# Moving a feed-forward's opening into the attention before it, and turning a recurrence's first batches from resident tokens

## The chip, the cores and the metric

The kernel runs on one core of a Trainium2 chip. Its engines are TensorE (PE; its weight loads are listed as PEld), VectorE (DVE), ScalarE (ACT), GpSimd (POOL) and SyncE (SP), which issues most transfers. Each engine runs its own queue in order; they meet only through semaphores. The metric is the time of one execution on the device in microseconds; the median of the timed runs counts. A span is the time from the first to the last instruction of the profiled execution, and times in rows count from its start.

## The reference

A decoder of two layers over 8 batches of 256 tokens with 256 columns, f32. Each of six steps is added to its input and layer-normalised:

```python
x = _layernorm(x + _L0_attn_ref(x, ...))    # window attention
x = _layernorm(x + _L0_xattn_ref(x, ctx, ...))   # first cross attention, 77 context tokens
x = _layernorm(x + _L0_ffn_ref(x, ...))     # eight experts, one for each token
x = _layernorm(x + _L1_attn_ref(x, ...))    # convolution of 4 taps, gates, recurrence
x = _layernorm(x + _L1_xattn_ref(x, ctx, ...))   # second cross attention
x = _layernorm(x + _L1_ffn_ref(x, ...))     # feed-forward with binarised weights
```

The steps that matter here:

```python
# recurrence, its start:
gi = jnp.einsum('btd,hd->bth', x, W_in)
gate, xc = jnp.split(gi, 2, axis=-1)
# feed-forward (bw = mean|w| * sign(w) for each output):
h = jax.nn.gelu(jnp.einsum('bsd,hd->bsh', x, bw1) + b1, approximate=False)
out = jnp.einsum('bsh,dh->bsd', h, bw2) + b2
```

## The kernel before, in words

All tokens stay in SBUF in one tensor, X (in rows: tokens), 16 tiles of 128 tokens, two tiles (TPB) for each batch. Six stages run one after the other, each a block with its own program for each engine. A block ends when all engines have ended; only then does the next one's work begin. A matmul needs its contraction dimension on the partitions, so every stage first transposes a batch on PE, against an identity matrix, into PSUM. A product of f32 precision is made of f16 passes: a value is scaled, its rounded half is written by ACT ("high", names ending in h) and the rest by DVE ("low", ending in l).

**The experts leave their results in DRAM** (slots). The recurrence (L2163) gathers them by token: POOL's `fetch(b, par)` issues two indirect DMAs (L2286) into y. DVE's `enter(b, par)` (L2428) adds them to X and takes the statistics, POOL's `root_in` the root, and `enter_norm` writes the normalised tokens back to X, counting `norm_in.ln_done`. POOL's order at the start is fetch(0), fetch(1), root_in(0), root_in(1), fetch(2).

**The recurrence's opening.** SP's `stage(b, par)` (L2257) waits for `ln_done` of that batch and copies its two tiles from X to a buffer xs by DMA; `stage(0, 0)` and `stage(1, 1)` stand first, then `next_loads(sp)`, the four weight loads of the second attention (L838), then a loop over the other batches. PE: `turn(0, 0)` (L2552) transposes xs into one PSUM bank, ACT's `tokens` copies it out, `way_in(0)` (L2564) multiplies by w_in, ACT's `conv_input` (L2340) puts the result into padded, DVE's `convolve` (L2446) makes the convolution, and after `turn(1, 1)` the loop over batches starts. ACT begins the block with the four high parts of w_g (L2329). DVE makes the low parts (L2528, w_gl; each 128x1024 of w_g and w_gh), all four of them after enter and enter_norm of batches 0 and 1 and before `convolve(0, 0, 0)`.

**The attention's last batch.** `cross_attention` (L1018) goes through eight units a batch. In each, PE turns four heads' probabilities (`turn_probs`, L1315), ACT writes the high part (L1173) and the next unit's exponential (L1165), DVE the low part (L1216), PE weighs the values (`weigh`, L1329). At the end of a tile DVE takes a reciprocal (L1223) and normalises, PE transposes ("heads", L1286), ACT copies (L1158), PE multiplies by the output weights ("mix", L1291), DVE adds the residual (L1233) and takes statistics, POOL the root (L155), DVE writes X (L159). In the last batch units 5 to 7 have no next batch to prepare. There, and at named places behind the last unit ("weighed", "heads", "mix", "last"), `cross_attention` calls an object `follow`, which may put the next stage's first work into the score banks (`spare`) and the banks of turned probabilities (`turned`). The first attention's follow is `RouteStart`, the router's opening: it transposes pairs of tiles, writes their halves and multiplies. The second attention's is `Nothing`, whose methods are empty.

**The feed-forward's opening.** `binary_ffn` (L2689): SP `stage(0, 0)`, `stage(1, 1)` (L2746), then reloads when `x_turned` and `xb_ready` allow. POOL's `add_bias` (L2779) adds b2 to a batch's two tiles. PE: `turn(0, 0)` and `turn(1, 1)` (L2889) into one bank x_bank, the second after DVE's low part of the first; `way_up(0, 0)` (L2902): four banks of eight f16 passes of 128x256. ACT: `tokens` (L2798, high parts), `all_hidden(0, 0)`: Gelu (L2806) of each bank, then high parts of h (L2813). DVE: `tokens_low` (L2837), `low` (L2843). Then `all_batches`: PE's batch b is turn(b+2), way_up(b+1), way_down(b) (L2915, 32 passes); DVE's is tokens_low(b+2), two lows of b+1, `residual(b, ·)` (L2850, L2855) for two tiles, two more lows, and the two writes of y.

Of the kernel before, what the change touches and what calls it, by code (L numbers as in the profile page):

```python
# [993 lines left out]


class Nothing:


    def add_buffers(self, ctx, nc, tag):
        pass  # L1000

    def load(self, sp):
        pass

    def gpsimd(self, pool, X):
        pass

    def scalar(self, act, place, spare, turned, out):
        pass

    def vector(self, dve, place, spare):
        pass

    def tensor(self, pe, place, X, norm, spare, turned, out, ident):
        pass
# [1147 lines left out]
def recurrence(nc, gates, slots, slot, ident, half, X, next_loads, cross, ctx_dram):  # L2163


    with ExitStack() as ctx:
# [86 lines left out]
        def _(sp):  # L2253
# [5 lines left out]
            stage(0, 0)  # L2259
            stage(1, 1)  # L2260
# [158 lines left out]
        def _(dve):  # L2419
# [103 lines left out]
            for b in (0, 1):  # L2523
                enter(b, b)
                enter_norm(b)
            for j in range(HT):
                dve.wait_ge(g_high, j + 1)
                dve.scalar_tensor_tensor(out=w_gl[:, j], in0=w_g[:, j], scalar=SCALE, in1=w_gh[:, j],  # L2528
                                         op0=ALU.mult, op1=ALU.subtract).then_inc(g_low, 1)
            dve.wait_ge(cleared, 1)  # L2530
# [11 lines left out]
        def _(pe):  # L2542
            pe.wait_ge(gates.w_loaded, 48)

            def turn(b, par):

                pe.wait_ge(staged[par], 8 * (b - par) + 16)
                if not first(b):
                    pe.wait_ge(x_ready, b)
                for g in range(KT_):  # L2550
                    for t in range(TPB):
                        ins = pe.transpose(x_bank[:, g, t * P:(t + 1) * P], xs[par][:, t, g * P:(g + 1) * P], ident[:])  # L2552
# [136 lines left out]
def binary_ffn(nc, weights, ident, half, X, out):  # L2689

    with ExitStack() as ctx:
# [9 lines left out]
        xb = [sb(f"xb{k}", [P, TPB, DIM]) for k in range(2)]  # L2701
        xh = [sb(f"xh{k}", [P, KT_, SEQ], F16) for k in range(2)]
        xl = [sb(f"xl{k}", [P, KT_, SEQ], F16) for k in range(2)]
        h = sb("h", [P, FT, SEQ])
        hh = [sb(f"hh{k}", [P, FT, SEQ], F16) for k in range(2)]
# [11 lines left out]
        xb_ready = sem("xb_ready")  # L2717
        x_turned = sem("x_turned")
        x_high = sem("x_high")
        x_low = sem("x_low")  # L2720
        up = sem("up")
        h_ready = sem("h_ready")
        h_high = sem("h_high")
# [20 lines left out]
        def _(sp):  # L2744
# [14 lines left out]
            stage(0, 0)  # L2759
            stage(1, 1)  # L2760
            restage(0, 0)
            restage(1, 1)
# [10 lines left out]
        def _(pool):  # L2773
            def add_bias(b, par):
                pool.wait_ge(staged[par], 8 * (b - par) + 16)
                if not (isinstance(b, int) and b < 2):
# [258 lines left out]
```

## Time and profile before

| | us |
|---|---|
| median of 3 runs | 1252.14 (1252.08 to 1253.18) |
| the profiled execution, its own run | 1253.59 |
| its span | 1251.9 |
| PE busy | 1069.3 (85%) |
| DVE busy | 958.7 (77%) |
| ACT busy | 693.1 (55%) |
| POOL busy | 385.7 (31%) |

The rows come from one profiled execution. A row of a timeline is: start, duration, engine, line, operation, the tiles it writes and reads, their sizes, how many instructions were merged (x4), and in brackets the idle time before it and what ended that. Matmuls overlap: the distance between two starts tells their rate, the printed duration includes the last one's way out. An SP row merges issues that follow each other, so its duration tells little. The granted clock of TensorE is given as a share: 1.00 is 2.4 GHz, 0.50 is 1.2 GHz.

### The profile page before, as it was taken

The numbers are of one execution on the slowest core, as the hardware profiler recorded it, in microseconds if no ns is written. First come the engines' busy times: TensorE is split into PE (matmuls) and PEld (weight loads), VectorE is DVE, ScalarE is ACT, GpSimd is POOL, SyncE is SP. The second block draws the span as 40 slices with busy tenths as digits, with TensorE's granted clock in tenths as the row PEclk, the third lists the DMA queues.
The fourth block names the chain that finished last, engine by engine and source line by source line (L and its number), as shares of the span: only waits on it lengthen the run. The fifth ranks groups of instructions, "written<-read, shape, count | busy, mean of one in ns | idle before, by whom it ended". The sixth has DMA issues, their size and how long they took to land. (4 is left out here: it accounts for less than half of the span.)

```text
span 1251.9 us, 30100 instructions
## 1 busy us (share of the span) xinstructions
PE 1069.3 (85%) x10763; PEld 856.2 (68%) x10763; DVE 958.7 (77%) x2126; ACT 693.1 (55%) x1461; POOL 385.7 (31%) x538
## 2 busy tenths in 40 slices
PE   4899999999999799985379998489999669998696
PEld 3578878778777577764357776477788557776585
DVE  7588878877887598897838783669998659988397
ACT  2354444544555265555637775368788626555484
POOL 5023222222221255651310000523431326555132
PEclk9899999999999899996579999699999969999799
DMA  7000000200000320005515521300000000000011
GB/s 261 8 11 2 10 13 2 83 3 2 2 2 2 117 89 23 11 9 229 202 53 186 189 97 52 113 18 26 25 9 21 1 14 23 23 15 5 35 53 49
DMA packets 34071, 65.34 MB, mean 52 GB/s; under 512 B 7590, under 2 KB 23334, under 8 KB 30886
## 3 DMA queue, kind: packets, MB, share of 16 engines
q1 hardware_dynamic: 32422, 59.62, 13.5%
q0 software_dynamic: 1536, 4.20, 1.0%
q8 instruction: 73, 1.20, 0.4%
q14 instruction: 40, 0.33, 0.1%
HBM read 43.03 MB, written 12.39 MB: 44 GB/s over the span
## 5 line engine op out<-in xcount | busy, mean ns | idle before, releaser
L1173 ACT ACTIVATE ca_pth<-ca_turned 77x512 f16<-77x512 f32 x128 | 75.9, 593 | 101.7 <-PE ca_turned L1315 101.7
L395 ACT ACTIVATE wa_probs<-wa_scores,wa_minus_top 128x192 f32<-128x192 f32 x256 | 83.3, 437 | 80.8 <-DVE wa_minus_top L488 80.8
L1116 POOL TENSOR_TENSOR ca_z<-ca_z,ca_top 128x308 f32<-128x308 f32 x128 | 88.1, 701 | 113.5 <-DVE ca_top L1211 113.5
L351 POOL TENSOR_TENSOR wa_q<-wa_by_cos,wa_by_sin 128x256 f32<-128x256 f32 x32 | 23.4, 732 | 266.5 <-DVE wa_by_sin L483 266.5
L1216 DVE SCALAR_TENSOR_TENSOR ca_ptl<-ca_turned,ca_pth 77x512 f16<-77x512 f32 x128 | 87.0, 680 | 21.4 <-ACT ca_pth L1173 21.4
L1315 PE MATMUL ca_turned<-ident,ca_probs 128*77 128x128 f32 x512 | 87.0, 294 | 14.3 <-ACT ca_probs L1165 13.8
L406 ACT ACTIVATE wa_pth<-wa_turned 128x384 f16<-128x384 f32 x128 | 58.4, 506 | 72.2 <-PE wa_turned L715 72.2
L1315 PEld LDWEIGHTS ca_turned<-ident,ca_probs 128*77 128x77 f32 x512 | 57.4, 151 | 44.9 <-ACT ca_probs L1165 24.5
L640 PE MATMUL wa_scores<-wa_xh,wa_wh 128*128 128x256 f16 x256 | 70.4, 275 | 11.2 <-DVE wa_wl L467 9.1
L488 DVE TENSOR_REDUCE wa_minus_top<-wa_scores 128x2 f32<-128x384 f32 x128 | 62.3, 548 | 20.9 <-PE wa_scores L703 18.9
L715 PE MATMUL wa_turned<-ident,wa_probs 128*128 128x128 f32 x512 | 68.3, 275 | 7.8 <-ACT wa_probs L395 3.9
L1165 ACT ACTIVATE ca_probs<-ca_z 128x308 f32<-128x308 f32 x128 | 57.7, 451 | 23.2 <-POOL ca_z L1116 23.2
L640 PE MATMUL wa_scores<-wa_xl,wa_wh 128*128 128x256 f16 x256 | 70.5, 275 | 0.0
L640 PE MATMUL wa_scores<-wa_xh,wa_wl 128*128 128x256 f16 x256 | 70.5, 275 | 0.0
L536 DVE SCALAR_TENSOR_TENSOR wa_ptl<-wa_turned,wa_pth 128x384 f16<-128x384 f32 x128 | 64.9, 548 | 6.6 <-ACT wa_pth L406 6.6
L2580 PE MATMUL re_g<-re_convh,re_w_gh 128*128 128x256 f16 x256 | 69.8, 273 | 0.0
L2580 PE MATMUL re_g<-re_convl,re_w_gh 128*128 128x256 f16 x256 | 69.8, 273 | 0.0
L2580 PE MATMUL re_g<-re_convh,re_w_gl 128*128 128x256 f16 x256 | 69.8, 273 | 0.0
L2564 PE MATMUL re_in<-re_xt,re_w_in 128*128 128x256 f32 x256 | 61.8, 403 | 9.0 <-ACT re_xt L2333 9.0
L715 PEld LDWEIGHTS wa_turned<-ident,wa_probs 128*128 128x128 f32 x512 | 57.6, 141 | 15.4 <-issue 6.7
L2564 PEld LDWEIGHTS re_in<-re_xt,re_w_in 128*128 128x128 f32 x256 | 51.1, 202 | 18.8 <-issue 7.2
L2011 DVE SCALAR_TENSOR_TENSOR ex_hl<-ex_h,ex_hh 128x320 f16<-128x320 f32 x72 | 35.2, 488 | 37.5 <-ACT ex_h L1983 36.8
(368 smaller groups left out, 3649.4 us busy)
## 6 DMA issues: line engine op xcount, KB each, us to landing
ex_stage<-in_ew SPq DMA_DIRECT2D x16, 1024.0 KB, 6.8
slots<-slots_zeros SPq DMA_DIRECT2D x10, 512.0 KB, 6.1
ca_xs<-tokens SPq DMA_DIRECT2D x16, 256.0 KB, 2.4
ex_xe<-slots SPq DMA_DIRECT2D x11, 320.0 KB, 3.2
slots<-ex_y SPq DMA_DIRECT2D x9, 320.0 KB
wa_x_stage<-in_xt SPq DMA_DIRECT2D x8, 256.0 KB, 3.1
tokens<-in_x SPq DMA_DIRECT2D x1, 2048.0 KB, 15.3
ca_w<-in_xw SPq DMA_DIRECT2D x2, 1024.0 KB, 6.4
```

What stands on the lines that cost most here:

```text
L395: ins = act.activation(probs[2 * (u % 2) + t][:, h, t * WINDOW:t * WINDOW + SPAN], s_bank[i][:, t * SPAN:(t + 1) * SPAN], ACT.Exp, bias=mi ...
L406: act.activation(spans(pth[k][:]), spans(t_bank[h][:]), ACT.Copy, scale=PSCALE).then_inc(probs_high, 1)
L488: dve.tensor_reduce(minus_top[:, g % 2, i], s_bank[i][:, 0:2 * SPAN].rearrange("p (t s) -> p t s", t=2), AX.X, ALU.max, negate=True).then_ ...
L536: dve.scalar_tensor_tensor(out=spans(ptl[k][:]), in0=spans(t_bank[h][:]), scalar=PSCALE, in1=spans(pth[k][:]), op0=ALU.mult, op1=ALU.subtr ...
L640: ins = pe.matmul(bank[:, a * SEQ:(a + 1) * SEQ], weight[:, k, cols], x[:, par, k], start=(m == 0), stop=(m == 3 * KT_ - 1))
L715: ins = pe.transpose(t_bank[h][:, j * SEQ + t * P:j * SEQ + (t + 1) * P], probs[2 * (u % 2) + t][:, h, j * P:(j + 1) * P], ident[:])
L1116: pool.tensor_tensor(z[k][:, heads], z[k][:, heads], top[:, k, heads].unsqueeze(2).broadcast_to((P, UH, CTX)), ALU.subtract).then_inc(shif ...
L1173: act.activation(pth[k][0:CTX], t_bank[k][0:CTX], ACT.Copy, scale=PSCALE).then_inc(probs_high, 1)
L1216: dve.scalar_tensor_tensor(out=ptl[k][0:CTX], in0=t_bank[k][0:CTX], scalar=PSCALE, in1=pth[k][0:CTX], op0=ALU.mult, op1=ALU.subtract).then ...
L1315: ins = pe.transpose(t_bank[k][0:CTX, h * P:(h + 1) * P], probs[k][:, h], ident[:])
L2564: ins = pe.matmul(i_bank[s % 2][:, k], w_in[:, g, m * P:(m + 1) * P], xt[:, g], start=(g == 0), stop=(g == KT_ - 1))
L2580: ins = pe.matmul(g_bank[m][:, k], w[:, j, cols], x[par][:, j], start=(n == 0), stop=(n == 3 * HT - 1))
```

## The change

Three things.

1. **Recurrence.** PE transposes batches 0 and 1 directly from X, waiting for `norm_in.ln_done`; their two loads go. SP waits for the fourth `ln_done` before `next_loads`. On DVE three of the four low parts of w_g come before enter(0), the fourth between batch 0 and batch 1.
2. **Second attention.** `Nothing` is replaced by `BinaryStart`, which does the feed-forward's opening in the attention's last batch: transposes, halves and biases of batches 0 and 1, the whole way_up(0), all_hidden(0).
3. **Feed-forward.** These steps go from its block. SP's first loads are those of batches 2 and 3; PE's first instruction is turn(2), DVE's are the four lows of batch 0.

```diff
@@ recurrence, sync
-            stage(0, 0)
-            stage(1, 1)
+            sp.wait_ge(norm_in.ln_done, 2 * TPB)
             next_loads(sp)
             with sp.Fori(1, BATCH // 2) as i:
@@ recurrence, vector
-            for b in (0, 1):
-                enter(b, b)
-                enter_norm(b)
-            for j in range(HT):
+            def weights_low(j):
                 dve.wait_ge(g_high, j + 1)
                 dve.scalar_tensor_tensor(out=w_gl[:, j], in0=w_g[:, j], scalar=SCALE, in1=w_gh[:, j],
                                          op0=ALU.mult, op1=ALU.subtract).then_inc(g_low, 1)
+
+            for j in range(3):
+                weights_low(j)
+            enter(0, 0)
+            enter_norm(0)
+            weights_low(3)
+            enter(1, 1)
+            enter_norm(1)
@@ recurrence, tensor
             def turn(b, par):
 
-                pe.wait_ge(staged[par], 8 * (b - par) + 16)
+                early = isinstance(b, int) and b < 2
+                if early:
+                    pe.wait_ge(norm_in.ln_done, (b + 1) * TPB)
+                else:
+                    pe.wait_ge(staged[par], 8 * (b - par))
                 if not first(b):
                     pe.wait_ge(x_ready, b)
                 for g in range(KT_):
                     for t in range(TPB):
-                        ins = pe.transpose(x_bank[:, g, t * P:(t + 1) * P], xs[par][:, t, g * P:(g + 1) * P], ident[:])
+                        tile_in = X[:, b * TPB + t] if early else xs[par][:, t]
+                        ins = pe.transpose(x_bank[:, g, t * P:(t + 1) * P], tile_in[:, g * P:(g + 1) * P], ident[:])
@@ new
+class BinaryStart:
...
+    def gpsimd(self, pool, X):
+
+        for b in range(2):
+            for t in range(TPB):
+                ins = pool.tensor_tensor(self.xb[b][:, t], X[:, b * TPB + t], self.weights.b2[:], ALU.add)
+            ins.then_inc(self.xb_ready, 1)
+
+    def hidden(self, act, s, bank):
+        act.wait_ge(self.up, s + 1)
+        for k in range(2):
+            m = 2 * s + k
+            ins = act.activation(self.h[:, m], bank[:, k], ACT.Gelu, scale=self.weights.alpha1[:, m:m + 1],
+                                 bias=self.weights.b1[:, m:m + 1])
+        ins.then_inc(self.h_ready, 1)
+
+    def high(self, act, s):
+        act.wait_ge(self.h_ready, s + 1)
+        act.activation(self.hh[0][:, 2 * s:2 * s + 2], self.h[:, 2 * s:2 * s + 2], ACT.Copy, scale=HSCALE).then_inc(self.h_high, 1)
+
+    def scalar(self, act, place, spare, turned, out):
+        banks = spare + turned
+        if place == 5:
+            for b in range(2):
+                act.wait_ge(self.x_turned, b + 1)
+                act.activation(self.xh[b][:], spare[b], ACT.Copy, scale=SCALE).then_inc(self.x_high, 1)
+        elif place == 7:
+            self.hidden(act, 0, banks[0])
+        elif place == "last":
+            for s in range(1, 4):
+                self.hidden(act, s, banks[s])
+                self.high(act, s - 1)
+            self.high(act, 3)
+
+    def vector(self, dve, place, spare):
+        if place == 6:
+            for b in range(2):
+                dve.wait_ge(self.x_high, b + 1)
+                dve.scalar_tensor_tensor(out=self.xl[b][:], in0=spare[b], scalar=SCALE, in1=self.xh[b][:],
+                                         op0=ALU.mult, op1=ALU.subtract).then_inc(self.x_low, 1)
+
+    def way_up(self, pe, s, bank):
+        sign1 = self.weights.sign1
+        for k in range(2):
+            m = 2 * s + k
+            n = 0
+            for x in (self.xh[0], self.xl[0]):
+                for g in range(KT_):
+                    ins = pe.matmul(bank[:, k], sign1[:, g, m * P:(m + 1) * P], x[:, g], start=(n == 0), stop=(n == 2 * KT_ - 1))
+                    n += 1
+        ins.then_inc(self.up, 1)
+
+    def tensor(self, pe, place, X, norm, spare, turned, out, ident):
+
+        if place == 5:
+            for b in range(2):
+                pe.wait_ge(norm.ln_done, (b + 1) * TPB)
+                for g in range(KT_):
+                    for t in range(TPB):
+                        ins = pe.transpose(spare[b][:, g, t * P:(t + 1) * P], X[:, b * TPB + t, g * P:(g + 1) * P], ident[:])
+                ins.then_inc(self.x_turned, 1)
+        elif place == 7:
+            pe.wait_ge(self.x_low, 1)
+            self.way_up(pe, 0, spare[0])
+        elif place == "weighed":
+            pe.wait_ge(self.x_low, 2)
+            self.way_up(pe, 1, spare[1])
+        elif place == "heads":
+            self.way_up(pe, 2, turned[0])
+        elif place == "mix":
+            self.way_up(pe, 3, turned[1])
@@ binary_ffn, sync
-            stage(0, 0)
-            stage(1, 1)
-            restage(0, 0)
-            restage(1, 1)
+            stage(2, 0)
+            stage(3, 1)
@@ binary_ffn, gpsimd
-            add_bias(0, 0)
-            add_bias(1, 1)
             all_batches(batch)(pool)
@@ binary_ffn, scalar
-            tokens(0, 0)
-            tokens(1, 1)
-            all_hidden(0, 0)
             all_batches(batch)(act)
@@ binary_ffn, vector
-            tokens_low(0, 0)
-            tokens_low(1, 1)
             for s in range(4):
                 low(0, 0, s)
             all_batches(batch)(dve)
@@ binary_ffn, tensor
-            turn(0, 0)
-            turn(1, 1)
-            way_up(0, 0)
             all_batches(batch)(pe)
@@ build
-        cross_attention(nc, start1, ins["context"], ident, half, X, Nothing())
-        binary_ffn(nc, binary, ident, half, X, out)
+        start2 = BinaryStart(ctx, nc, binary)
+        cross_attention(nc, start1, ins["context"], ident, half, X, start2)
+        binary_ffn(nc, start2, ident, half, X, out)
```

## Rows read from the trace of the kernel before

**Rows 1.** Busy time by stage: stretch, length, busy us of each engine, clock, DMA
```profile
1182.00:1252.00 70.00, 57.97 (x499) 48.74 (x497) 57.80 (x149) 46.73 (x96) 20.80 (x28) 0.97 0.13 46
```

**Rows 2.** Timeline of the recurrence's opening on DVE, SP and PE
```profile
790.49 0.42 DVE L2428 TENSOR_TENSOR rn_res<-re_y,tokens 128x256 f32<-128x256 f32 x1 [4.76 <-DMA re_y<-slots,re_where]
...
793.76 0.41 DVE L159 TENSOR_SCALAR tokens<-rn_res,rn_mv,rn_rstd 128x256 f32<-128x256 f32 x1 [0.45 <-POOL rn_rstd L155]
...
797.89 4.62 DVE L2528 SCALAR_TENSOR_TENSOR re_w_gl<-re_w_g,re_w_gh 128x1024 f16<-128x1024 f32 x4
803.03 0.42 DVE L2446 TENSOR_SCALAR re_conv<-re_padded,re_hid 128x256 f32<-128x256 f32 x1 [0.52 <-ACT re_padded L2340]
...
794.20 4.34 SPq L2257 DMA_DIRECT2D re_xs<-tokens  x2
...
796.73 1.09 PE L2552 MATMUL re_x<-ident,re_xs 128*128 128x128 f32 x4 [18.22 <-DMA re_xs<-tokens]
```

**Rows 3.** The same timeline on ACT and POOL
```profile
785.72 3.89 ACT L2329 ACTIVATE re_w_gh<-re_w_g 128x1024 f16<-128x1024 f32 x4 [8.40 <-POOL re_tiny L2271]
...
787.75 0.97 POOL L2286 DMA_INDIRECT re_y<-slots,re_where  x1 [0.30 <-issue]
...
797.89 1.27 POOL L2277 TENSOR_TENSOR re_carry<-half 128x1 f32<-128x1 f32 x1
799.32 1.84 POOL L2286 DMA_INDIRECT re_y<-slots,re_where  x1 [0.16 <-issue]
```

**Rows 4.** Timeline of the second attention's last batch on PE and DVE
```profile
1154.66 0.66 PE L1315 MATMUL ca_turned<-ident,ca_probs 128*77 128x128 f32 x4 [0.74 <-ACT ca_probs L1165]
...
1163.12 0.66 PE L1286 MATMUL ca_shared<-ident,ca_o 128*128 128x128 f32 x2 [2.52 <-DVE ca_o L1227]
1164.35 2.05 PE L1291 MATMUL ca_shared<-ca_w,ca_ot 128*128 128x256 f32 x4 [0.56 <-ACT ca_ot L1158]
...
1166.43 0.42 DVE L1233 TENSOR_TENSOR ca_res<-ca_shared,ca_xb 128x256 f32<-128x256 f32 x1 [3.46 <-PE ca_shared L1291]
...
1168.39 0.41 DVE L159 TENSOR_SCALAR tokens<-ca_res,ca_mv,ca_rstd 128x256 f32<-128x256 f32 x1 [0.66 <-POOL ca_rstd L155]
```

**Rows 5.** The same of the first attention, whose last batch carries RouteStart
```profile
560.71 0.66 PE L1315 MATMUL ca_turned<-ident,ca_probs 128*77 128x128 f32 x4 [0.74 <-ACT ca_probs L1165]
...
569.03 0.25 DVE L1223 RECIPROCAL ca_inv<-ca_out 128x16 f32<-128x16 f32 x1
...
572.34 0.41 DVE L1233 TENSOR_TENSOR ca_res<-ca_shared,ca_xb 128x256 f32<-128x256 f32 x1
```

**Rows 6.** PE alone: stretch, length, busy (count), granted clock, DMA share, GB/s
```profile
568.00:570.00 2.00, 0.47 (x5) 1.00 0.00 0
1163.00:1164.00 1.00, 0.66 (x2) 0.50 0.00 0
1179.00:1180.00 1.00, 1.00 (x8) 0.69 0.00 0
798.50:804.20 5.70, 5.69 (x14) 0.50 0.77 281
```

**Rows 7.** Timeline of the feed-forward's opening on SP, POOL, PE and DVE
```profile
1170.16 6.58 SPq L2746 DMA_DIRECT2D bf_xs<-tokens  x4
...
1172.54 2.76 POOL L2779 TENSOR_TENSOR bf_xb<-bf_xs,bf_b 128x256 f32<-128x256 f32 x4 [4.19 <-DMA bf_xs<-tokens]
...
1186.34 1.04 PE L2915 MATMUL bf_out<-bf_sign,bf_hl 128*128 128x256 f16 x8
1187.22 1.04 PE L2915 MATMUL bf_out<-bf_sign,bf_hh 128*128 128x256 f16 x8
...
1189.49 0.42 DVE L2850 TENSOR_TENSOR bf_scaled<-bf_out,bf_alpha 128x256 f32<-128x256 f32 x1
```

**Rows 8.** ACT from 1170 on, grouped by line: total busy, mean ns, idle before
```profile
L2806 ACT ACTIVATE bf_h<-bf_up,bf_b,bf_alpha 128x256 f32<-128x256 f32 x64 | 32.3, 582 | 3.0 <-PE bf_up L2902 2.7 <-DVE bf_hl L2843 0.3
L2813 ACT ACTIVATE bf_hh<-bf_h 128x512 f16<-128x512 f32 x32 | 19.9, 656 | 0.0
```

More of the change, by code:

```diff
@@ L993, in first_product @@
         self.multiply(pe, shared, ident, 0, 0, kind, *self.opening(kind))
[L996 to L1015, printed above, removed]
 def cross_attention(nc, start, ctx_dram, ident, half, X, follow, next_loads=None, table=None):
@@ L2686, in load, with __init__, sb, sem @@
             sp.dma_start(tile[:], dram).then_inc(self.loaded, 16)
-def binary_ffn(nc, weights, ident, half, X, out):
+class BinaryStart:
+    def __init__(self, ctx, nc, weights):
+        def sb(name, shape, dt=F32):
+            return ctx.enter_context(nc.sbuf_tensor("bf_" + name, shape, dt))
+        def sem(name):
+            return ctx.enter_context(nc.semaphore("bf_" + name))
+        self.weights = weights
+        self.xb = [sb(f"xb{k}", [P, TPB, DIM]) for k in range(2)]
+        self.xh = [sb(f"xh{k}", [P, KT_, SEQ], F16) for k in range(2)]
+        self.xl = [sb(f"xl{k}", [P, KT_, SEQ], F16) for k in range(2)]
+        self.h = sb("h", [P, FT, SEQ])
+        self.hh = [sb(f"hh{k}", [P, FT, SEQ], F16) for k in range(2)]
+        self.xb_ready = sem("xb_ready")
+        self.x_turned = sem("x_turned")
+        self.x_high = sem("x_high")
+        self.x_low = sem("x_low")
+        self.up = sem("up")
+        self.h_ready = sem("h_ready")
+        self.h_high = sem("h_high")
+    def add_buffers(self, ctx, nc, tag):
+        pass
+    def load(self, sp):
+        pass
+    def gpsimd(self, pool, X):
[60 more added lines that the diff above has]
+            self.way_up(pe, 3, turned[1])
@@ L2691, in binary_ffn @@
+def binary_ffn(nc, start, ident, half, X, out):
+    weights = start.weights
     with ExitStack() as ctx:
@@ L2700, in binary_ffn @@
         xs = [sb(f"xs{k}", [P, TPB, DIM]) for k in range(2)]
[L2701 to L2705, printed above, removed]
+        xb, xh, xl, h, hh = start.xb, start.xh, start.xl, start.h, start.hh
         hl = [sb(f"hl{k}", [P, FT, SEQ], F16) for k in range(2)]
@@ L2716, in binary_ffn @@
         stored = [sem("stored0"), sem("stored1")]
[L2717 to L2723, printed above, removed]
+        xb_ready, x_turned, x_high, x_low = start.xb_ready, start.x_turned, start.x_high, start.x_low
+        up, h_ready, h_high = start.up, start.h_ready, start.h_high
         h_low = sem("h_low")
@@ L2774, in add_bias @@
             def add_bias(b, par):
-                pool.wait_ge(staged[par], 8 * (b - par) + 16)
-                if not (isinstance(b, int) and b < 2):
-                    pool.wait_ge(summed, (b - 1) * TPB)
+                pool.wait_ge(staged[par], 8 * (b - par))
+                pool.wait_ge(summed, (b - 1) * TPB)
                 for t in range(TPB):
@@ L2883, in turn @@
             def turn(b, par):
-                pe.wait_ge(staged[par], 8 * (b - par) + 16)
-                if not first(b):
-                    pe.wait_ge(x_low, b)
+                pe.wait_ge(staged[par], 8 * (b - par))
+                pe.wait_ge(x_low, b)
                 for g in range(KT_):
```

## The prediction

> **How the profile was read.** First the busy shares of a full stretch: in the feed-forward's last 70 us DVE works 57.8 and PE 58.0 [rows 1]. The change leaves such stretches alone; it touches two seams, where all engines wait. So I read every engine's timeline around each seam, then the granted clock there, and last the end of the first attention, whose last batch already carries a follow-on opening (the router's): it shows what such a fill costs.
>
> **The seam into the recurrence, now.** DVE idles until 790.49, when the gathered rows of batch 0 have landed. It normalises them (last write of X 793.76 + 0.41 = 794.17); only then SP issues the load that copies X into xs, and PE's first transpose follows at 796.73. From there it is a chain: PE, ACT, way_in on PE, ACT, and the convolution on DVE at 803.03, which waited for ACT [rows 2].
>
> **The change there.** PE now waits for ln_done itself: 796.73 - 794.17 = 2.56 us go, less about 0.1 for an engine's semaphore (the convolution starts 0.1 after ACT's output), so 2.4 are to be had. The other edits:
> - Two loads leave SP; its queue then waits for the fourth ln_done and issues the next stage's four loads, some 2 us later than now. Nothing needs them before the recurrence's end, some 200 us on; I cost this at nothing. Were that cover gone, it would cost those 2 us.
> - DVE runs three of the four weights_low before enter(0). Four take 4.62 us [rows 2], so one 1.155. ACT has the first input ready after a quarter of its 3.89, at 786.7 [rows 3]; the three occupy 786.8 to 790.3, inside DVE's idle time, so DVE itself loses nothing. But POOL is then issuing the gathers on which enter(0) waits. Today these run beside an idle DVE, the second in 0.97. Beside these very weights_low a gather takes 1.84, and a one-column POOL addition that starts with the first of them 1.27 [rows 3], about as long as the DVE instruction. So weights_low hold POOL off. I price both gathers of batch 0 at the disturbed duration: 2 x (1.84 - 0.97) = 1.7 us. Today the second ends at 788.72 and DVE starts 1.77 later; that becomes 790.4 and 792.2. The root of batch 0 stands on POOL behind batch 1's gathers, which run beside an idle DVE again; two at 0.97 with their small steps are some 3 us, until 793.4, and about then its input is ready. I add nothing for it. DVE's 3.68 (790.49 to 794.17) give ln_done at 795.9, PE at 796.0.
> So PE starts 2.4 - 1.7 = **0.7 us** earlier. Bounds: gathers whose work on POOL's side is done before 786.8 or slips between leave the full 2.4; POOL held until the third conversion ends at 790.3, with the rest of the second gather behind it (up to 0.9), gives 791.1, a delay of 2.4 and no gain. I take the value in between because it is the duration measured beside the same instruction.
> - The fourth conversion and batch 1 follow on DVE, 1.2 + 3.7, until 800.8; the convolution's input comes at 802.3: covered, 1.5 us to spare. PE wants batch 1 only behind way_in(0). Behind this everything is the same chain, shifted.
>
> The Trainium skill, "SBUF — State Buffer", section "SBUF: two separate sides", says that a VectorE instruction with two SBUF inputs and a GpSimd instruction take their shared ports as an exclusive lock, and that a DMA issued from GpSimd lacks its descriptors meanwhile. The 1.27 and 1.84 of [rows 3] agree. Taken strictly, it makes rival 2 below of this seam.
>
> **The seam into the feed-forward, now.** The second attention's last write of X ends at 1168.39 + 0.41 = 1168.80 [rows 4]. SP issues the first load 1.36 later, and it lands 2.38 behind that: POOL's addition, which waits for it as PE does, starts at 1172.54 [rows 7]. Then come turn(0), ACT, DVE, turn(1) and way_up(0), mostly at half clock. DVE is first without gaps from residual(0,0) on, 1189.49 [rows 7]; behind it DVE sets the pace. I measure the gain at that instruction.
>
> **The change there.** T is the turn of unit 5's probabilities, 1154.66 [rows 4].
> - Eight transposes, two ACT copies and two DVE splits enter units 5 and 6. The first attention carries the same fill and one pair of steps more: its reciprocal runs at T + 8.32 (569.03 - 560.71) and PE's heads of tile 1 would follow some 0.85 behind, at T + 9.2 [rows 5]; in the second, without fill, heads run at T + 8.46 (1163.12) [rows 4]. That is +0.7; with a pair less I take +0.4, heads at 1163.5.
> - way_up(0) and way_up(1), 16 f16 passes at 0.109 (eight are 0.88 apart [rows 7]) = 1.75 us, fit between 1160 and 1162.5, where PE now idles. Cover gone, they would add their 1.75.
> - The clock. Now it is 0.50 in 1163 to 1164, after 2.5 us of PE without work, and mix(1) runs 2.05 us. With the router's fill the first attention reads 1.00 in 568 to 570 though PE works only 0.47 of 2 us [rows 6]. I take full clock: way_up(2) starts 0.25 behind heads, until 1164.6 (ACT's copy of heads is done about 1164.4, so 0.2 is the cost), mix(1) then takes half of 2.05, and residual(1) starts at 1165.8 instead of 1166.43 [rows 4]. The first attention has it at T + 11.63 (572.34) [rows 5], the second at T + 11.77.
> - ACT: a table load (1.28 now beside PE's work) moves into idle time behind the last exponential. Behind the copy at 1164.4 stand six Gelus and four copies: 6 x 32.3/64 + 4 x 19.9/32 = 5.5 us [rows 8], until 1169.9.
> - POOL: the root is done 1.95 behind residual(1)'s start (1168.39 against 1166.43), at 1167.75, and behind it stand the four additions, 2.76 us [rows 7], formerly beside PE's work: 1170.5. POOL now ends the block: **+1.7 us** against 1168.80.
> - The load's wait isn't removed: PE's first work is turn(2), from a load issued at the block's start. 1170.5 + 1.36 + 2.38 = 1174.2 for PE, and way_up(1) at 1175.1. DVE's four splits of batch 0 run under the load.
> - Half clock: PE then has idled since 1166.6. Now it comes back inside 1179 to 1180, some 6.9 us behind turn(0) with a pause of 1.5 in between; in the recurrence it was at half for the 5.7 us from way_in's start at 798.5 on [rows 6]. Without a pause I take 1179.1, between 1178.5 and 1180. way_up(1)'s 32 passes: 4.0/0.218 = 18 at half, 14 at 0.109, done 1180.6. way_down(0)'s first tile, 16 passes, 1.75: residual(0,0) at 1182.4. ACT's and DVE's splits of batch 1 follow PE's pace and are just ready.
> So 1189.49 - 1182.4 = **7.1 us**, 6.4 to 7.5 by the clock's return. Behind residual(0,0) PE has about 6 us for a turn and 64 passes less a tile; 5.5 are needed. It just holds.
>
> **Sum.** 0.7 + 7.1 = 7.8 us. Profiled: span 1251.9, its run 1253.59, so 1244.1 and 1245.8. That run lies 1.45 above the median of 1252.14, so the median goes to 1244.3.
>
> **Rivals.**
> 1. Gathers not held off: 2.4 + 7.1 = 9.5, 1242.6. For it: the first gather starts before the first conversion. Against: [rows 3].
> 2. Gathers held until the third conversion has ended: 0 + 7.1, 1245.0. For it: the 1.27 that lasts as long as the DVE instruction. Against: a gather of 1.84 spans two of them and isn't held for both.
> 3. The tail falls to half clock as now: way_up(2) 1.75 and mix(1) 2.05 end the block 2.0 later, 5.8 are left, 1246.3; with rival 2, 1247.0. Against: the 1.00 of [rows 6].
> 4. The opening only changes place: the tail grows by what the block loses, 7 us. 1252. The first attention's tail speaks against.
> 5. Slower: PE stays at half clock into the feed-forward's loop. A batch's 64 passes and 4 transposes then take 15 us instead of some 8 (70 us for eight batches and the last one's tail). Each us at half costs PE half a us; the gain is gone once half clock lasts 15.6 us longer than I say, until 1194.7; lasting until 1204 it gives 1256.8. For it: PE's idle time ahead of the block grows from 6.1 to 7.6. Against: no busy stretch here stays at half beyond some 7 us, and the loop reads 0.97 [rows 1].
>
> The Trainium skill, "TensorE: Matmul & The Clock Gate", section "HAM oscillation — how this bites in real kernels", tells of a kernel whose DMA waits keep the clock low throughout. By that, rival 5 would come true, as each turn here waits for a load.
>
> **Chances.** Forecast 0.45, rivals 1 to 5: 0.15, 0.20, 0.12, 0.04, 0.04. The range reaches to rivals 1 and 3 with about 1 us for sizes taken from neighbouring rows: 1241.5 to 1248.0. 0.2% (2.5 us) is about what a measurement of this kernel can tell from no change: faster 0.92, same 0.04, slower 0.04.
>
> **What will show it.** Right: enter(0) near 792.2 and gathers of 1.8; PE's first transpose of the recurrence near 796.0; clock 1.00 up to mix(1); POOL's additions last in the attention's block; residual(0,0) 7 us earlier relative to the recurrence. Wrong: gathers of 1.0, a mix(1) of 2.05, gaps on DVE behind residual(0,0), or a recurrence longer than before because the moved loads collide with its gathers.

## The result, and the profile after

The changed kernel takes 1242.74 us in the median (1241.62 to 1243.73) beside 1252.66 (1252.08 to 1253.81) for the kernel before: a ratio of 0.9919, 95% interval 0.9902 to 0.9937. The profiled execution has a span of 1242.0; before, 1251.9. That is 9.9 us less, where 7.8 were forecast.

**Where it came from.** Take four marks in both traces: POOL's first instruction of the recurrence's block (its start, below), T, the turn of unit 5 in the second attention's last batch (1154.66 before [rows 4], 1151.45 after), residual(0,0), and the end.

| stretch | before | after | gain |
|---|---|---|---|
| first instruction to the recurrence's block | 785.59 | 786.28 | -0.69 |
| recurrence's block to T | 369.07 | 365.17 | 3.90 |
| T to residual(0,0) | 34.83 | 28.13 | 6.70 |
| residual(0,0) to the end | 62.41 | 62.42 | -0.01 |

The first line is code that the change doesn't touch; "The free part", further down, returns to it.

**The seam into the recurrence, after.** The timeline of POOL, DVE and PE; the columns are those of [rows 2] and [rows 3], which these lines answer.

```profile
787.12 1.01 POOL L2263 DMA_INDIRECT re_y<-slots,re_where  x1 [0.32 <-issue]
788.43 1.13 POOL L2263 DMA_INDIRECT re_y<-slots,re_where  x1 [0.30 <-issue]
...
789.98 1.06 POOL L2254 TENSOR_TENSOR re_carry<-half 128x1 f32<-128x1 f32 x1
...
793.45 1.11 POOL L155 TENSOR_TENSOR rn_rstd<-rn_var_eps,half 128x1 f32<-128x1 f32 x2
...
787.50 3.49 DVE L2502 SCALAR_TENSOR_TENSOR re_w_gl<-re_w_g,re_w_gh 128x1024 f16<-128x1024 f32 x3 [1.08 <-ACT re_w_gh L2306]
791.41 0.43 DVE L2405 TENSOR_TENSOR rn_res<-re_y,tokens 128x256 f32<-128x256 f32 x1 [0.42 <-DMA re_y<-slots,re_where]
...
794.09 0.93 DVE L159 TENSOR_SCALAR tokens<-rn_res,rn_mv,rn_rstd 128x256 f32<-128x256 f32 x2 [0.18 <-POOL rn_rstd L155]
...
801.45 0.98 DVE L2423 TENSOR_SCALAR re_conv<-re_padded,re_hid 128x256 f32<-128x256 f32 x2 [1.71 <-ACT re_padded L2317]
...
795.16 1.08 PE L2539 MATMUL re_x<-ident,tokens 128*128 128x128 f32 x4 [15.96 <-DVE tokens L159]
```

The gathers of batch 0 take 1.01 and 1.13, not 1.84. enter(0), the first of DVE's residual additions, follows 5.13 us behind the block's start (before: 4.90), and PE's idle time now ends on DVE's write of X, not on a DMA: 8.88 behind the start, before 11.14.

TensorE's granted clock behind that, with PE's own work (stretch, length, busy and count, clock, DMA share, GB/s):

```profile
796.00:798.00 2.00, 1.31 (x5) 0.50 0.00 0
798.00:801.00 3.00, 3.00 (x9) 0.50 0.02 1
801.00:803.00 2.00, 2.00 (x11) 1.00 0.81 217
```

PE is at half clock for 4.1 us from way_in's start (796.93) on; in the kernel before it was for 5.7 [rows 6].

**The seam into the feed-forward, after.** PE, POOL, SP and DVE; it answers [rows 4] and [rows 7].

```profile
1160.28 0.41 PE L1264 MATMUL ca_shared<-ident,ca_o 128*128 128x128 f32 x2 [1.17 <-DVE ca_o L1205]
...
1161.40 1.03 PE L1269 MATMUL ca_shared<-ca_w,ca_ot 128*128 128x256 f32 x4
...
1171.00 1.11 PE L2959 MATMUL bf_x<-ident,bf_xs 128*128 128x128 f32 x4 [7.70 <-DMA bf_xs<-tokens]
...
1177.63 1.04 PE L2985 MATMUL bf_out<-bf_sign,bf_hh 128*128 128x256 f16 x8
...
1163.84 0.55 POOL L155 TENSOR_TENSOR ca_rstd<-ca_var_eps,half 128x1 f32<-128x1 f32 x1 [4.78 <-DVE ca_var_eps L150]
1164.35 2.81 POOL L2710 TENSOR_TENSOR bf_xb<-tokens,bf_b 128x256 f32<-128x256 f32 x4
...
1168.61 1.15 SPq L2827 DMA_DIRECT2D bf_xs<-tokens  x2
...
1162.46 0.42 DVE L1211 TENSOR_TENSOR ca_res<-ca_shared,ca_xb 128x256 f32<-128x256 f32 x1 [2.33 <-PE ca_shared L1269]
...
1179.58 0.42 DVE L2923 TENSOR_TENSOR bf_scaled<-bf_out,bf_alpha 128x256 f32<-128x256 f32 x1 [0.32 <-PE bf_out L2985]
```

mix(1) (L1269) runs in 1.03, half of its 2.05 before. POOL's four additions end last in the block, at 1167.16 (1164.35 + 2.81); the first load follows 1.45 behind, PE 2.39 behind that. PE's granted clock beside it, in the columns of [rows 6]:

```profile
1160.00:1162.00 2.00, 1.72 (x13) 1.00 0.00 0
1162.00:1164.00 2.00, 1.30 (x10) 1.00 0.00 0
1164.00:1166.00 2.00, 0.00 (x0) 1.00 0.00 0
1166.00:1168.00 2.00, 0.00 (x0) 0.56 0.00 0
```

The 70 us that end the run, which answer [rows 1], hold the same kind of work as before, with the opening's half clock now inside them:

```profile
1172.00:1242.00 70.00, 59.58 (x501) 50.46 (x499) 56.08 (x146) 44.56 (x90) 20.77 (x28) 0.94 0.13 46
```

So the feed-forward's seam gave 6.7 where 7.1 was forecast, and the recurrence 3.9 where 0.7 was. The experiments go after that.

### The profile page after: what moved, and what is told of

Read it like the earlier page. It is cut to its first block and busy times, and to the rows that moved or that the text cites. A ratio compares the mean times of both kernels' runs of the same rounds, so it can differ in the third digit from the quotient of the medians.

```text
span 1242.0 us, 30094 instructions
## 1 busy us (share of the span) xinstructions
PE 1065.2 (86%) x10763; PEld 854.6 (69%) x10763; DVE 960.4 (77%) x2126; ACT 692.5 (56%) x1461; POOL 382.7 (31%) x538
```

## The experiments

Each ran beside the kernel before on the same chip; ratios are to that kernel. Besides the median, each is read by the marks above, and by "PE's start": the recurrence's first transpose, counted from its block's start.

### The two seams apart

`rec_only` is the kernel before with the changed recurrence, `ff_only` the kernel before with the changed tail and feed-forward, `after_again` the changed kernel unchanged.

> Only the recurrence's part of the change (turn from X, conversions ahead, loads later). Theory A, a shifted chain: PE's first transpose of the recurrence comes 2.3 us earlier relative to the block's first instruction, and the median falls by 2.3 us, to about 1250.3. Theory B, the clock decides: the start moves by 2.3 as well, but where PE's clock falls in the recurrence moves with it, and the time falls by 2.3 plus or minus 1 to 2 us (one dip more or less). My forecast's own price, 0.7 us, would give 1251.9; the trace of the changed kernel already speaks against it.

> Only the feed-forward's opening in the attention's last batch, the recurrence as before. Theory A: 6.7 us less by the trace of the changed kernel (7.1 as forecast), about 1245.9. If the two parts just add up, rec_only and ff_only together give the whole 9.9 us; a sum that misses by over 1 us means that a part of the gain is neither's own, but the clock's.

> The changed kernel once more, unchanged. If PE's clock falls at fixed places of the program, the falls at 828 to 836 and none at 976 to 988 come again and the span is 1242.0 within 0.3. If they depend on something outside of the program, a fall may come or go, and the span differs by 1 to 2 us; the runs of either kernel lay 1.7 to 2.1 us apart.

| | median | ratio (95%) | PE's start | block to T | T to residual |
|---|---|---|---|---|---|
| before | 1252.61 | | 11.14 | 369.07 | 34.83 |
| rec_only | 1248.23 | 0.9968 (0.9958 to 0.9979) | 8.88 | 365.44 | 34.87 |
| ff_only | 1245.15 | 0.9937 (0.9924 to 0.9949) | 11.31 | 368.75 | 28.11 |
| after_again | 1243.18 | 0.9919 (0.9906 to 0.9932) | 8.88 | 365.36 | 28.12 |

The marks add up: the one half brings 3.6 ahead of T, the other 6.7 behind it, and each leaves the other's stretch alone to within 0.3. The medians, -4.4 and -7.5, add to -11.8 beside the -9.4 of both. That misses by 2.4 us, more than the 1 us that the expectation of `ff_only` allows; but the intervals are 1.3 to 1.6 us either way on each of the three, so the medians can't decide that question. It is the marks that show that neither seam takes from the other.

`rec_only` brings 3.6 at T where a shifted chain (its theory A) would bring 2.3, so a part of this seam's gain is more than the earlier start. `after_again` answers its own question for the recurrence: PE's work lost to half clock near 828 (the table further down shows how it is counted) was 2.8 us in the first trace and 3.0 in the second, and none was lost near 980 in either. The same holds for `rec_only`, `adds_first` and `both_tail`, which leave the changed recurrence as it is (2.7 to 3.1, and none). Their stretch from the block to T is 365.2 to 365.5. The span was 1241.5, 0.5 off where 0.3 was allowed, since the block started 0.7 sooner.

### The order on DVE alone

```diff
@@ reorder_only: kernel before, recurrence, vector; the two loads stay
+            for j in range(3):
+                weights_low(j)
+            enter(0, 0)
+            enter_norm(0)
+            weights_low(3)
...
```

> The kernel before with DVE's new order alone: three conversions of w_g ahead of enter(0), the fourth between the batches; PE still turns from loaded copies. Theory A (a POOL instruction waits only until the DVE instruction that runs at its start has ended): the first two gathers take 1.0 and 1.1 us, DVE's enter(0) starts 5.1 us behind the block's first POOL instruction instead of 4.9, and the time is unchanged within 0.3 us. Forecast's price (each gather 1.84): enter(0) at 6.6, and 1.7 us slower, 1254.3.

Measured 1252.0, ratio 0.9998 (0.9989 to 1.0006): no change. Its gathers take 1.01 and 1.13, enter(0) comes 5.06 behind the block's start, PE's start at 11.30. Put the other way round, the changed kernel with DVE's old order:

```diff
@@ old_order: kernel after, recurrence, vector
+            for b in (0, 1):
+                enter(b, b)
+                enter_norm(b)
+            for j in range(HT):
...
```

> The changed kernel with DVE's old order in the recurrence: enter 0 and 1 first, then all four conversions. PE still turns from X. Theory A (the start is what counts, DVE's order is a side matter): gathers undisturbed, enter(0) 0.2 us sooner behind the block's first POOL instruction (4.9), PE's first transpose at 8.7 instead of 8.9. But the four conversions (4.6 us) then end 17.0 behind the block's first instruction, where the convolution's input comes at 15.1: DVE late by 1.8 there; whether PE feels it depends on its own 7 us of way_in(1) in front of the first gate product. Predicted: 0 to 1.5 us slower than the changed kernel, 1243 to 1244.5. Rival (the order costs what I forecast, 1.7): 1.5 us faster, 1241.3.

1241.21, ratio 0.9919 (0.9905 to 0.9932), the same as with the new order. enter(0) comes at 4.90 and PE's start at 8.73, 0.23 and 0.15 sooner than in the changed kernel. The loss of 0 to 1.5 us that was expected didn't come: block to T is 364.87 beside 365.17. The rival's number, 1241.3, was met, but not its reason, which was 1.7 us at enter(0). The order on DVE costs some 0.2 us at enter(0), not 1.7, and no gain from it shows; the earlier start comes from transposing from X, as long as the loads stay late (below).

### Why the gathers aren't held

```diff
@@ quarters: kernel after, recurrence, vector, weights_low(j)
+                for c in range(4):
+                    cols = slice(c * HID // 2, (c + 1) * HID // 2)
+                    ins = dve.scalar_tensor_tensor(out=w_gl[:, j, cols], in0=w_g[:, j, cols], scalar=SCALE, in1=w_gh[:, j, cols],
+                                                   op0=ALU.mult, op1=ALU.subtract)
```

> The changed kernel with each conversion of w_g cut into four of 256 columns (about 0.35 us each instead of 1.22). Theory A (a POOL instruction waits for the DVE instruction that runs at its start, and for no more): POOL's one-column addition, 1.06 us now, takes at most 0.6, and the second gather, 1.13, is back at about 1.0; the third gather starts 0.5 us sooner or more. Rival (a GpSimd instruction is slowed by DVE's traffic in general, however it is cut): the addition stays near 1.1 and the gathers above 1.1. The time is within 0.5 us of the changed kernel either way.

1241.02, ratio 0.9911 (0.9896 to 0.9927). POOL's timeline, to be laid beside that of the changed kernel above:

```profile
785.80 1.00 POOL L2263 DMA_INDIRECT re_y<-slots,re_where  x1 [0.30 <-issue]
786.81 0.21 POOL L2259 COPY re_where<-slot 128x2 int32<-128x2 int32 x1
787.10 0.27 POOL L2254 TENSOR_TENSOR re_carry<-half 128x1 f32<-128x1 f32 x1
787.51 1.00 POOL L2263 DMA_INDIRECT re_y<-slots,re_where  x1
```

With DVE's instructions a quarter as long (twelve in 4.12 us, 784.87 to 788.99), the one-column addition takes 0.27 instead of 1.06 and the second gather 1.00 instead of 1.13. The third starts 3.86 behind the block's start instead of 4.91 and takes 1.00. DVE reads and writes the same amount in both kernels, so the rival, a general slowing, is out. POOL thus waits for the end of the one DVE instruction that runs when it starts, and not for the ones behind it. With that, the durations fall in place from the rows: the addition at 789.98 ends (791.04) with the third conversion (787.50 + 3.49 = 790.99). A gather needs some 0.85 to 0.95 behind the conversion that it meets: the second one of the changed kernel starts at 788.43, the first conversion ends about 788.7, the gather at 789.56. The 1.84 of [rows 3] started at 799.32, 0.9 before the end (800.2) of a conversion, and so took 0.9 + 0.95. The first gather starts 0.38 ahead of the first conversion and isn't touched. The loss is set by where in a conversion a gather starts, and the second one here happens to start near an end.

### The loads that were put behind a wait

```diff
@@ loads_first: kernel after, recurrence, sync
-            sp.wait_ge(norm_in.ln_done, 2 * TPB)
             next_loads(sp)
```

> The changed kernel with the second attention's four weight loads (2.2 MB) issued at the start of the recurrence's block instead of behind the fourth normalised tile. My forecast costed their place at nothing, because nothing waits for them. Theory A: they now share the transfer engines with the first gathers, whose landing (1.8 us behind the second gather's end) grows by 1 to 4 us; enter(0) and PE's first transpose come that much later and so does the end, 1244 to 1247. Rival (place is free): 1243.

1245.77, ratio 0.9948 (0.9932 to 0.9963). Timeline of SP, DVE and PE:

```profile
786.55 1.86 SPq L838 DMA_DIRECT2D ca_w<-in_xw  x1
...
794.12 0.42 DVE L2404 TENSOR_TENSOR rn_res<-re_y,tokens 128x256 f32<-128x256 f32 x1 [3.74 <-DMA re_y<-slots,re_where]
...
797.95 1.09 PE L2538 MATMUL re_x<-ident,tokens 128*128 128x128 f32 x4 [19.37 <-DVE tokens L159]
```

Its gathers are issued as in the changed kernel (1.01, 1.13), yet DVE waits 3.74 for them instead of 0.42: the block's start to enter(0) is 8.46 beside 5.13, PE's start 12.29 beside 8.88. The four loads (1.9 MB), issued in the same microseconds, delay the landing of the gathered rows by 3.3. How busy the DMA engines were just then (last but one column: their busy share; last: GB/s), first in `loads_first`, then in the changed kernel:

```profile
787.00:794.00 7.00, 0.00 (x0) 0.50 0.88 311
```

```profile
787.00:794.00 7.00, 0.00 (x0) 0.50 0.20 59
```

The delay takes nearly the whole gain of the recurrence: from its block to T 368.76, before 369.07, after 365.17. In the kernel before, the two loads of batches 0 and 1 stood ahead of `next_loads` on SP and kept them late by the way. The wait that the change adds on SP keeps that up, and is thus not a detail but a condition of the gain at this seam; the forecast had looked only at what a later load could cost, not at what an earlier one would.

### The start of the recurrence, later by a known amount

```diff
@@ delay1 (range(2)) and delay2 (range(4)): kernel after, recurrence, scalar, tokens(0)
+                if first(b):
+                    for k in range(2):
+                        act.activation(dump[k][:], x_bank[:], ACT.Copy)
                 act.activation(xt[:], x_bank[:], ACT.Copy).then_inc(x_ready, 1)
```

Two or four more copies on ACT, between the first transposes and way_in(0), make the opening 1.0 and 2.0 us longer (measured: way_in's start goes from 10.65 to 11.64 and 12.62 behind the block's start).

> The changed kernel with two extra copies (about 0.5 us each, 1.0 us together) on ACT ahead of the copy of the first turned batch in the recurrence: its chain starts 1.0 us later, everything else is the same. Theory A, a rigid chain: every later mark of the recurrence is 1.0 later (last product with the gate at 215.3 behind the block's first POOL instruction instead of 214.3). Theory B, the clock takes part: where PE's clock falls (824 to 836, or 976 to 988, or both) changes with the start, and the last mark moves by 1.0 plus or minus 1 to 2 us, so anything from 213.5 to 217.

> The same with four extra copies, 2.0 us later. Theory A: the last product with the gate at 216.3, PE's turn of batch 1 at 21.7. Theory B: a shift other than 2.0 at the last mark; since the kernel before starts 2.3 later than the changed one and has no long fall at 828 but one at 980, this one should look like it: 216.5 to 217.9.

| | median | ratio (95%) | way_in | half clock behind it | turn(1) | T |
|---|---|---|---|---|---|---|
| before | 1253.35 | | 12.92 | 5.7 | 22.70 | 369.07 |
| after | | | 10.65 | 4.1 | 19.66 | 365.17 |
| delay1 | 1241.07 | 0.9905 (0.9888 to 0.9922) | 11.64 | 3.4 | 20.30 | 365.43 |
| delay2 | 1246.45 | 0.9949 (0.9933 to 0.9966) | 12.62 | 5.8 | 22.47 | 368.90 |

The marks are microseconds behind the block's start; "half clock behind it" is how long PE stays at half clock from way_in's start on. The row "after" is the first trace of the changed kernel. One us of delay leaves T 0.3 later, two leave it 3.7 later; a rigid chain (theory A) is refuted by both. The 0.3 is no more than scatter: five executions of the unchanged recurrence lie between 365.17 and 365.45. Nor does delay1's ratio differ from that of the changed kernel, 0.9919 (0.9902 to 0.9937).

All fourteen traces together show a step and no slope. In the nine with way_in at 10.5 to 11.6, T comes at 364.8 to 366.1; in the five with way_in at 12.6 to 14.1 (delay2, before, `ff_only`, `reorder_only`, `loads_first`), at 368.3 to 369.1. `loads_first` starts way_in 1.4 later than delay2, and its T is 0.1 sooner.

Part of where that comes from stands in PE's granted clock, in four-microsecond stretches. The kernel before:

```profile
828.00:832.00 4.00, 0.43 (x1) 0.93 0.00 0
832.00:836.00 4.00, 4.00 (x13) 0.64 0.00 0
...
980.00:984.00 4.00, 2.43 (x6) 0.71 0.00 0
984.00:988.00 4.00, 4.00 (x17) 0.87 0.00 0
```

The changed kernel:

```profile
828.00:832.00 4.00, 2.79 (x7) 0.54 0.00 0
832.00:836.00 4.00, 4.00 (x13) 0.61 0.00 0
...
980.00:984.00 4.00, 3.69 (x17) 1.00 0.00 0
```

delay1:

```profile
824.00:828.00 4.00, 0.85 (x5) 1.00 0.00 0
828.00:832.00 4.00, 4.00 (x20) 1.00 0.00 0
...
976.00:980.00 4.00, 4.00 (x12) 0.57 0.00 0
```

delay2:

```profile
828.00:832.00 4.00, 1.26 (x3) 0.84 0.00 0
832.00:836.00 4.00, 4.00 (x15) 0.74 0.00 0
...
980.00:984.00 4.00, 3.22 (x8) 0.61 0.00 0
```

At several places PE comes out of a pause, and finds its clock at half or doesn't: way_in, a pause near 828, one near 980, and the change to the attention's block (992 to 1028). A kernel that arrives at another moment finds other falls there. The work that PE loses is its busy time times the missing clock. Behind way_in that is half of the length at half clock; elsewhere it is summed over stretches of 4 us:

| | way_in | near 828 | near 980 | 992 to 1028 | sum |
|---|---|---|---|---|---|
| before | 2.8 | 1.5 | 1.2 | 6.6 | 12.1 |
| after | 2.1 | 2.8 | 0 | 6.4 | 11.3 |
| delay1 | 1.7 | 0 | 1.7 | 7.3 | 10.7 |
| delay2 | 2.9 | 1.2 | 1.4 | 6.9 | 12.4 |

Against the changed kernel, delay1 pays 1.0 and gets 0.6 back: 0.4, where T shows 0.3. delay2 pays 2.0 and 1.1 more: 3.1, where T shows 3.7. The kernel before starts PE 2.3 later and loses 0.8 more: 3.1, where T shows 3.9. By this sum the falls account for a good part of what is more than the delay itself; 0.6 and 0.8 stay open. `loads_first` fits too: 3.4 later at way_in, 0.1 more lost from the block's start to T, 3.6 at T. So does `quarters`: it has both falls (2.7 near 828, 1.6 near 980), and its T comes 0.9 later with way_in only 0.2 later. What makes a fall come or stay away at a given arrival isn't shown.

### POOL's additions ahead of the last root

```diff
@@ adds_first: kernel after, cross_attention, gpsimd
-            norm.root(pool, BATCH - 1, 1)
             follow.gpsimd(pool, X)
+            norm.root(pool, BATCH - 1, 1)
```

> The changed kernel with POOL's four bias additions (2.8 us) ahead of the root of the last tile instead of behind it; they need only tokens that are long final. Theory A (POOL ends the attention's block, as forecast): the block then ends with ACT's last copy, 1.25 us sooner (1165.91 against 1167.16 in the changed kernel's trace), the first load of the feed-forward is issued 1.2 us sooner, and the time falls by about 1.2, to 1241.8. Rival (something else ends the block, or PE's clock eats it): no change.

1241.58, ratio 0.9917 (0.9903 to 0.993). The additions now run while PE still works, and ACT's last two copies end the block, at 1162.94 (1161.76 + 1.18), as expected; DVE's last write is done at 1161.85:

```profile
1155.64 2.83 POOL L2710 TENSOR_TENSOR bf_xb<-tokens,bf_b 128x256 f32<-128x256 f32 x4
1160.85 0.55 POOL L155 TENSOR_TENSOR ca_rstd<-ca_var_eps,half 128x1 f32<-128x1 f32 x1 [2.38 <-DVE ca_var_eps L150]
...
1161.76 1.18 ACT L2723 ACTIVATE bf_hh<-bf_h 128x512 f16<-128x512 f32 x2
```

SP's first load comes 16.25 behind T instead of 17.16: 0.9 sooner, so the additions did end the block. (1.25 was expected, from 1167.16 to the end of ACT's copies at 1165.91. But the additions now run beside DVE's write of tile 0's tokens, which takes 0.81 instead of 0.41, and everything behind it comes 0.4 later.) residual(0,0) comes 2.0 sooner (26.12 beside 28.13), the rest because half clock behind it costs less, 1.5 us of lost PE work between 1164 and 1172 beside 2.7 between 1168 and 1178 in the changed kernel; 0.9 are given back behind (63.31 beside 62.42 to the end). The 1.1 left are less than the medians can tell here.

### A version that takes both

`both_tail` has POOL's additions first and takes batches 2 and 3 of the feed-forward from X too, for PE's transposes and POOL's additions; `best` also has DVE's old order.

```diff
@@ both_tail, binary_ffn (adds_first's edit as well)
-            stage(2, 0)
-            stage(3, 1)
...
+                early = isinstance(b, int) and b < 4
+                if not early:
+                    pe.wait_ge(staged[par], 8 * (b - par) - 16)
...
+                        tile_in = X[:, b * TPB + t] if early else xs[par][:, t]
```

> Bias additions ahead of the last root, and batches 2 and 3 of the feed-forward turned (PE) and biased (POOL) from X instead of from loaded copies. Theory A (the load's 2.4 us is what PE waits for at the block's start): PE's first transpose comes 1.4 instead of 3.8 us behind the block's end, and residual(0,0) at 15.4 to 15.8 behind the first reciprocal of the last batch instead of 17.75 with the additions moved alone; behind it DVE was no longer full in that run (63.3 instead of 62.4 to the end), so 1 to 2 us of the 2.4 reach the end: 1239.5 to 1240.5. Rival (DVE and ACT, or half clock, take it all): 1241.5.

> The same with DVE's old order in the recurrence on top. Old order alone ran 1241.2 against 1243.0 of the changed kernel, and its last product with the gate came 1.0 sooner (213.3 against 214.3). Theory A: 1.0 less than with the new order, 1238.5 to 1239.5. Rival (that was where PE's clock fell in those executions, not the order): the same time as the tail edits alone.

`both_tail`: 1238.91, ratio 0.9892 (0.9872 to 0.9911). `best`: 1238.9, ratio 0.9885 (0.9869 to 0.9902). PE's first work of the feed-forward in both_tail:

```profile
1166.70 1.09 PE L2963 MATMUL bf_x<-ident,tokens 128*128 128x128 f32 x4 [4.04 <-PEq L1341]
```

It no longer waits for a DMA (idle 7.70 in the changed kernel, now 4.04) and follows 1.43 behind the last engine's end (1165.27, ACT's copies), as expected. residual(0,0) comes 24.77 behind T beside 28.13: 3.4 us, all of which reach the end (62.35), where 1 to 2 us of 2.4 had been expected on top of what `adds_first` gave. The ratio says about the same beside that of the changed kernel, 0.9919: 3.4 us, with an uncertainty hardly smaller than that. The median of `best` is that of `both_tail`, as its rival says. By the marks the old order is worth 0.4 us at residual(0,0) (389.80 behind the recurrence's block start, 390.22 in `both_tail`), not the 1.0 expected, and the medians can't tell either.

## Why the prediction was right, and where it missed

The time of 1242.74 lies in the range, 1.6 below the forecast of 1244.3, and the kernel is faster, as forecast.

**What the number owes to luck.** The span fell by 9.9 where 7.8 was forecast. The recurrence gave 3.2 more than its 0.7, the feed-forward 0.4 less, and 0.7 were lost ahead of both in untouched code. The 7.1 of the feed-forward carries the forecast; the recurrence's 0.7 by itself was off by a factor of five.

**The feed-forward's seam: right by its own steps.** 7.1 forecast, 6.7 measured, and 6.7 again in `ff_only`. Behind T: heads of tile 1 at 8.83 (said: 8.84), residual(1) at 11.01 (11.14), POOL's additions end at 15.71 (15.84), 1.57 later than the block's last write before (14.14; said: +1.7). PE's first work follows 3.84 behind (3.74). The 0.4 are at the end: the clock returned about 4.5 us behind way_up(1)'s start (4.0), and residual(0,0) came 1.95 behind way_down(0)'s start (1.75). The fill keeps the clock at 1.00 through mix(1), as the first attention's did [rows 6]: rival 3 is out. The span of 6.4 to 7.5 given for this term is wider than its own working: 0.6 and 0.9 us of half clock are worth 0.3 and 0.45, so 6.6 to 7.4.

**The recurrence's seam: the right mechanism, one term wrong.** The term is "both gathers of batch 0 at the disturbed duration: 2 x (1.84 - 0.97) = 1.7 us". Measured, 0.2: enter(0) came at 5.13 behind the block's start instead of the forecast's 6.6, PE's start 2.26 sooner instead of 0.7. Rival 1, with 2.4, describes this seam up to PE's start. That its 1242.6 is so close to the measured 1242.74 is in part luck, as T shows 3.9 here and not 2.4. The error was to carry a duration over without asking at which moment of DVE's instruction it had been taken. Both starts were in the rows: 799.32 inside a conversion, against gathers that would start at 786.42 and 787.75 beside conversions from 786.8 on. Had I asked how long the conversion still ran when each gather started, the answer would have been nothing for the first and some 0.2 for the second. The Trainium skill, "SBUF — State Buffer", section "SBUF: two separate sides", describes the shared ports as an exclusive lock, held for the whole of one instruction. `quarters` agrees: the wait ends with that instruction (1.06 against 0.27). Rival 2, which stretched the lock over all three conversions, is refuted by 1.13 and 1.06; that was my reading of it and goes beyond what the section says.

**The clock's part was missing.** I forecast "the same chain, shifted". The gain grows from 2.26 at PE's start to 3.04 at turn(1), since half clock behind way_in lasts 4.1 instead of 5.7 us (1.6 at half is 0.8), and to 3.9 at T. `delay1` and `delay2` show that this rest hangs on the moment at which PE's work starts; the falls in its clock make up a part of it, and some 0.8 stay unexplained. I see no way to have had its size from the rows of one execution.

**A cover costed at nothing.** SP's wait before the next loads was costed as a delay of 2 us that nothing needs. It is 0.5 (the first of them 13.49 behind the block's start, before 13.00). `loads_first` shows that the same edit spares 3.3 us of landing time for the gathers. The forecast came out right there only because the change put the loads late, for another reason than this.

**The slower rivals.** Rival 4 (the opening only changes place) is refuted by the tail: from T to SP's first load it grows by 1.7 (15.50 to 17.16), not 7. Rival 5 would need half clock until 1194; it lasts until about 1176.4, and residual(0,0) to the end takes 62.42 beside 62.41. The Trainium skill's account of a clock kept low by DMA waits ("TensorE: Matmul & The Clock Gate", section "HAM oscillation — how this bites in real kernels") doesn't apply to this loop.

**The free part.** The recurrence's block starts between 782.75 and 788.68 in the traces of all these kernels, though none changes what runs before it. The granted clock shows a reason: PE's lost work ahead of that block runs from 24.7 us in `adds_first` (start 782.75) to 31.1 in `rec_only` (788.65), about as much as the starts differ. Near 376 there is a fall of 1.2 to 2.8 us in `rec_only`, `ff_only` and `reorder_only`, the three that start last, and none in any other trace. In the pair compared here the start moved by 0.69, with 29.1 and 28.8 us lost, so the falls don't explain that one. A span alone is thus uncertain by some 3 us either way, and marks counted from a block's start are the better measure.

## What to carry to other kernels

Take the price of two engines in each other's way from where inside the other's instruction yours starts, not from a disturbed duration found elsewhere; and look at early bulk loads for whose landing they hold up, not only at who waits for them. A filled tail keeps TensorE's clock up to its last product, and once it is filled the smallest engine may end the block: put its off-path work ahead of its last on-path step. After a shift, expect later half-clock stretches to be dealt anew. Here the lost work changed by about 1 us either way, and the stretch's end came up to 1.7 us later than the shift alone would put it, or 0.7 sooner.

## What the runs showed of the hardware

- A POOL instruction that starts inside a DVE instruction with two SBUF inputs waits for that one's end and not for the next: an addition of one column took 1.06 beside DVE instructions of 1.2 us and 0.27 beside some a quarter as long (`quarters`); an indirect DMA's issue 1.13 and 1.00.
- Four loads (1.9 MB) issued in the same three microseconds as the gathers delayed the gathers' landing by 3.3 us (`loads_first`), with the DMA engines 0.88 busy instead of 0.20; POOL's part of the gathers took the same 1.01 and 1.13.
- 1.0 us more ahead of way_in cost nothing that can be told (0.3) some 360 us later, 2.0 us cost 3.7 (`delay1`, `delay2`).
- Executions of the same code lost about the same work to half clock in the recurrence (2.7 to 3.1 us near 828 and none near 980, five traces), but not always near 376 (none, or 1.2 to 2.8 us).
